# Transposed weights woven into the attention epilogue, and loads split into pieces: a pre-norm layer on eight cores

## What is computed

```python
x = x + attn(layernorm(x))     # x is [4, 4096, 1024] fp32
x = x + ffn(layernorm(x))

def attn(x, w_qkv, w_fc, b_fc, gamma, beta):
    q, k, v = split(x @ w_qkv.T)
    att = softmax(q @ k.T / 32)
    y = einsum('bqk,bvd->bqd', att, v)        # k and v are summed apart
    h = x + y @ w_fc.T + b_fc
    return layernorm(h) * gamma + beta

def ffn(x, w_gate, w_up, w_down):             # inner size 4096
    gate = silu(bitlinear(x, w_gate)); up = bitlinear(x, w_up)
    return bitlinear(gate * up, w_down)
# bitlinear: weights rounded to -1, 0, 1 times mean(|w|); activations to 8-bit integers per row
```

## Time and profile before

| | us |
|---|---|
| median of 2 runs | 4026.79 (4022.05 to 4031.53) |
| the profiled execution | 4026.35 |
| its span, slowest core (core 4) | 4024.8 |
| spans of the eight cores | 4006.8 to 4024.8 |
| VectorE busy | 1588.0 |
| TensorE busy | 856.0 |

### The profile page before, as it was taken

One profiled execution on the slowest core, in us unless ns is written; L12 is line 12 of the kernel. 1 busy time (PEld: TensorE's weight loads), 2 busy tenths in 40 slices (PEclk: granted clock), 3 DMA queues, 4 the chain that ended last, 5 costly groups with the idle time before them and its releaser, 6 DMA issues.

```text
span 4024.8 us, 21432 instructions; the slowest of 8 cores (4006.8 to 4024.8 us)
## 1 busy us (share of the span) xinstructions
PE 856.0 (21%) x3852; PEld 430.0 (11%) x3852; DVE 1588.0 (39%) x3100; ACT 278.4 (7%) x378; POOL 259.1 (6%) x392
## 2 busy tenths in 40 slices
PE   1222200000000300000000047019015900591066
PEld 1222200000000000000000013004002400240022
DVE  5555433333333100024447764713830373037400
ACT  0000000000000000000000023103100310031000
POOL 1111110000000000024430000000000000000000
PEclk9999999999999755555555568559558955895588
DMA  4444443335333475321111142044025402550244
GB/s 129 154 146 136 148 149 108 106 107 136 102 102 97 107 174 149 97 67 42 52 43 46 42 120 84 32 107 123 21 78 158 130 21 68 142 157 21 58 128 128
DMA packets 387523, 404.15 MB, mean 100 GB/s; under 512 B 240961, under 2 KB 306497, under 8 KB 383298
## 3 DMA queue, kind: packets, MB, share of 16 engines
q1 hardware_dynamic: 222210, 163.65, 15.0%
q10 hardware_dynamic: 149760, 176.19, 14.8%
q0 software_dynamic: 15424, 62.93, 4.1%
HBM read 251.67 MB, written 96.47 MB: 86 GB/s over the span
## 4 chain that ended last, share of the span: by engine, by line
DVE 33%; DMA 32%; PE 15%; issue 7%; SPq 6%; ACTq 3%; POOL 2%; DVEq 1%; ACT 1%; POOLq 0%
DVE AR L35 16%; PE pb L35 15%; DVE p0scr L35 7%; SPq L35 5%; DMA wstg<-w_down 5%; DMA wstg<-w_up 5%; DMA AR<-s_wd2t 5%; DMA wstg<-w_gate 4%; DVE svec L35 4%; DMA AR<-s_wd 3%; ACTq L35 2%; POOL AR L35 2%; DMA s_x<-AR 2%; DVE p0f L35 2%; DMA s_wd2t<-AR 2%
## 5 line engine op out<-in xcount | busy, mean ns | idle before, releaser
L35 PE MATMUL pb<-AR 128*128 128x512 bf16 (+1 forms) x3072 | 700.6, 386 | 1898.7 <-DMA AR<-s_wg2t 1222.5
L35 PEld LDWEIGHTS pb<-AR 128*128 128x128 bf16 (+1 forms) x3072 | 303.0, 99 | 2296.7 <-issue 1980.3
L35 DVE TENSOR_TENSOR AR<-AR 128x1024 f16<-128x1024 f16 (+2 forms) x464 | 295.5, 637 | 456.6 <-ACT AR L35 343.9
L35 DVE TENSOR_SCALAR p0scr<-wstg,tcols 128x1024 bf16<-128x1024 f32 x192 | 144.5, 753 | 456.1 <-DMA wstg<-w_down 159.8
L35 DVE SCALAR_TENSOR_TENSOR AR<-pb,a2d,AR 128x512 f32<-128x512 f32 x32 | 24.0, 750 | 496.7 <-PE pb L35 392.1
L35 PE MATMUL pb<-ones_cf,xstage 128*128 128x1 f32 x512 | 113.4, 351 | 362.2 <-DVE xstage L35 362.2
L35 DVE SCALAR_TENSOR_TENSOR p0f<-wstg 128x512 f32<-128x512 f32 x192 | 132.9, 692 | 102.8 <-DMA wstg<-w_down 30.2
L35 DVE SCALAR_TENSOR_TENSOR svec<-svec 128x1 f32<-128x1 f32 x96 | 16.3, 170 | 357.2 <-ACT svec L35 350.3
L35 PEld LDWEIGHTS pb<-ones_cf,xstage 128*128 128x128 f32 x512 | 111.6, 330 | 363.9 <-issue 363.9
L35 DVE TENSOR_SCALAR AR<-AR 128x1024 f16<-128x1024 f16 x320 | 136.6, 427 | 34.6 <-DVE AR L35 0.9
L35 DVE TENSOR_REDUCE svec<-AR 128x1 f32<-128x512 f16 (+1 forms) x160 | 126.8, 792 | 23.8 <-DMA AR<-s_x 7.1
(11 more groups left out here) (107 smaller groups left out, 737.8 us busy)
## 6 DMA issues: line engine op xcount, KB each, us to landing
wstg<-w_gate ACTq DMA_DIRECT2D x64, 512.0 KB, 3.6
wstg<-w_up ACTq DMA_DIRECT2D x64, 512.0 KB, 3.6
wstg<-w_down ACTq DMA_DIRECT2D x64, 512.0 KB, 4.0
AR<-s_wg2t SPq DMA_DIRECT2D x256, 128.0 KB, 2.6
AR<-s_wu2t SPq DMA_DIRECT2D x256, 128.0 KB, 2.9
AR<-s_wd2t SPq DMA_DIRECT2D x128, 256.0 KB, 2.6
AR<-x_full POOLq DMA_DIRECT2D x32, 512.0 KB, 6.2
AR<-s_x SPq DMA_DIRECT2D x32, 512.0 KB, 3.9
```

What stands on the lines that cost most here:

```text
L35: return getattr(E, meth)(*args, **kw)
```

## The change

Three things. First, stage 5 is no longer recorded ahead of the epilogue. A function `rt_emit(n)` records the next n of 64 items on ScalarE's queue, and it is called with 4 at the end of each of the 16 epilogue tiles. An item is half a gate or up block (2 transposes of [1024, 128], one 512 KB store) or one down block. Two slots are used in turn, with semaphores of their own (`qTR0/1` for the transposes, `qTS0/1` for the stores), and an item's first transpose waits for the store of the item two before. The waits on the finished weights become waits on both `qTS` counts. The load of the first activation transposes on SP waits for them too.

Second, each 512 KB load of the FFN weights (stages 1 and 3) and of w_qkv and w_fc (stage 2) becomes four DMAs of 256 columns, 128 KB each, on the same queue and the same semaphore. Third, each 512 KB load of x (stages 1 and 6) and of x1 (stage 7 and the end of each FFN block) becomes two DMAs of 512 columns. Stage 3, stage 2 and the x1 loads are changed as the two shown.

```diff
@@ -230,8 +230,13 @@
             waits = []
             if idx >= 2:
                 waits.append(("vV", p0b_abs[idx - 2]))
-            ld = b.dma("scalar", f"qA{slot}", mk("dma_start", out=stg, in_=w3_tile(m, j)),
-                       waits=waits)
+            src = w3_tile(m, j)
+            ld = None
+            for q4 in range(4):
+                ld = b.dma("scalar", f"qA{slot}",
+                           mk("dma_start", out=stg[:, q4 * 256:(q4 + 1) * 256],
+                              in_=src[:, q4 * 256:(q4 + 1) * 256]),
+                           waits=waits if q4 == 0 else ())
             aw = [(f"qA{slot}", ld)]
             if idx >= 2:
                 aw.append(("gC", 2 * (idx - 2) + 2))
...
@@ -336,8 +347,11 @@
             t_idx = g * 4 + i
             xt = AR4[:, i * 1024:(i + 1) * 1024]
             w = [("vV", e_norm_done[t_idx - 4])] if t_idx >= 4 else []
-            b.dma("gpsimd", "qP1X", mk("dma_start", out=xt,
-                                       in_=x_hbm[t_idx * 128:(t_idx + 1) * 128, :]), waits=w)
+            for q2 in range(2):
+                b.dma("gpsimd", "qP1X",
+                      mk("dma_start", out=xt[:, q2 * 512:(q2 + 1) * 512],
+                         in_=x_hbm[t_idx * 128:(t_idx + 1) * 128, q2 * 512:(q2 + 1) * 512]),
+                      waits=w if q2 == 0 else ())
         grp_total = b.cnt["qP1X"]
         for i in range(4):
             xt = AR4[:, i * 1024:(i + 1) * 1024]
...
@@ -534,36 +552,50 @@
         bank_gate[2 + eh] = ("vV", e_colfc)
     e_p2_tensor = b.cnt["tM"]
 
-    rtA = AR3[:, 5120:9216]
-    rtB = rtA[:, 0:1024].bitcast(F16)
-    e_rt_st = None
-    for mtx, src, dst in ((0, s_w3[0], s_wg2t), (1, s_w3[1], s_wu2t)):
-        for ds in range(8):
+    rt_slots = [AR3[:, 5120:7168], AR3[:, 7168:9216]]
+    rt_items = ([("gu", mtx, ds, half) for mtx in (0, 1) for ds in range(8)
+                 for half in range(2)] +
+                [("wd", ic, 0, 0) for ic in range(32)])
+    rt_state = {"i": 0, "st": {}}
+
+    def rt_emit(n):
+        while rt_state["i"] < len(rt_items) and n > 0:
+            i = rt_state["i"]
+            kind, a1, a2, a3 = rt_items[i]
+            sl = i % 2
+            slot = rt_slots[sl]
             lw = []
-            if mtx == 0 and ds == 0:
+            if i == 0:
                 lw += [("qAS0", e_qas_all[0]), ("qAS1", e_qas_all[1]),
                        ("tM", e_p2_tensor)]
-            if e_rt_st is not None:
-                lw.append(("qTR1", e_rt_st))
-            ldr = None
-            for q in range(4):
-                ldr = b.dma("scalar", "qTR0",
-                            mk("dma_start", out=rtA[:, q * 1024:(q + 1) * 1024],
-                               in_=src[q * 1024:(q + 1) * 1024, ds * 128:(ds + 1) * 128],
-                               transpose=True), waits=lw if q == 0 else ())
-            e_rt_st = b.dma("scalar", "qTR1",
-                            mk("dma_start", out=dst[ds * 128:(ds + 1) * 128, :], in_=rtA),
-                            waits=[("qTR0", ldr)])
-    e_rt_wgwu = e_rt_st
-    for ic in range(32):
-        ldr = b.dma("scalar", "qTR0",
-                    mk("dma_start", out=rtB, in_=s_w3[2][:, ic * 128:(ic + 1) * 128],
-                       transpose=True),
-                    waits=[("qTR1", e_rt_st)])
-        e_rt_st = b.dma("scalar", "qTR1",
-                        mk("dma_start", out=s_wd2t[ic * 128:(ic + 1) * 128, :], in_=rtB),
-                        waits=[("qTR0", ldr)])
-    e_rt_all = e_rt_st
+            if i >= 2:
+                lw.append((f"qTS{sl}", rt_state["st"][i - 2]))
+            if kind == "gu":
+                src = s_w3[a1]
+                dst = s_wg2t if a1 == 0 else s_wu2t
+                ldr = None
+                for q in range(2):
+                    ldr = b.dma("scalar", f"qTR{sl}",
+                                mk("dma_start", out=slot[:, q * 1024:(q + 1) * 1024],
+                                   in_=src[a3 * 2048 + q * 1024:a3 * 2048 + (q + 1) * 1024,
+                                           a2 * 128:(a2 + 1) * 128],
+                                   transpose=True), waits=lw if q == 0 else ())
+                st = b.dma("scalar", f"qTS{sl}",
+                           mk("dma_start",
+                              out=dst[a2 * 128:(a2 + 1) * 128, a3 * 2048:(a3 + 1) * 2048],
+                              in_=slot), waits=[(f"qTR{sl}", ldr)])
+            else:
+                sl16 = slot[:, 0:1024].bitcast(F16)
+                ldr = b.dma("scalar", f"qTR{sl}",
+                            mk("dma_start", out=sl16,
+                               in_=s_w3[2][:, a1 * 128:(a1 + 1) * 128],
+                               transpose=True), waits=lw)
+                st = b.dma("scalar", f"qTS{sl}",
+                           mk("dma_start", out=s_wd2t[a1 * 128:(a1 + 1) * 128, :],
+                              in_=sl16), waits=[(f"qTR{sl}", ldr)])
+            rt_state["st"][i] = st
+            rt_state["i"] += 1
+            n -= 1
 
     gbrow = fcB[0:1, 0:1024]
     e_gamld = b.dma("gpsimd", "qMB", mk("dma_start", out=gbrow, in_=gam_hbm[:, :]),
...
@@ -629,8 +661,12 @@
         xw = [("vV", e_cast_last)]
         if qt >= 2:
             xw.append(("vV", prev_ep[qt - 2]["x_done"]))
-        ld_x = b.dma("sync", f"qXT{qslot}",
-                     mk("dma_start", out=xt, in_=x_hbm[qt * 128:(qt + 1) * 128, :]), waits=xw)
+        ld_x = None
+        for q2 in range(2):
+            ld_x = b.dma("sync", f"qXT{qslot}",
+                         mk("dma_start", out=xt[:, q2 * 512:(q2 + 1) * 512],
+                            in_=x_hbm[qt * 128:(qt + 1) * 128, q2 * 512:(q2 + 1) * 512]),
+                         waits=xw if q2 == 0 else ())
         lw = [(f"qXT{qslot}", ld_x), ("vV", e_fcbc)]
         ev_ln1t = b.op("vector", mk("tensor_scalar", ln1t, xt, mu1[:, qt:qt + 1], r1c[:, qt:qt + 1],
                                     Alu.subtract, Alu.mult), inc="vV", waits=lw)
...
@@ -675,7 +711,11 @@
         b.dma("gpsimd", "qGX1", mk("dma_start", out=s_x1[qt * 128:(qt + 1) * 128, :], in_=hbuf),
               waits=[("vV", ev_x1)])
         prev_ep[qt] = {"x_done": ev_x1}
-
+        rt_emit(4)
+
+    rt_emit(64)
+    e_rt_wgwu = [("qTS0", rt_state["st"][30]), ("qTS1", rt_state["st"][31])]
+    e_rt_all = [("qTS0", rt_state["st"][62]), ("qTS1", rt_state["st"][63])]
     e_p3_tensor = b.cnt["tM"]
     e_p3_v = b.cnt["vV"]
     e_p3_g = b.cnt["gP"]
...
@@ -764,7 +808,7 @@
             ed5 = b.dma("gpsimd", "qMB", mk("dma_start", out=s_dbg[:, 4096:5120], in_=g2b))
             b.wait("vector", "qMB", ed5)
         b.op("vector", mk("scalar_tensor_tensor", g1b, g1b, -1.0, g2b, Alu.add, Alu.add), inc="vV")
-        qw2 = [("qGQ1", 16 * tt)] if tt >= 1 else [("qTR1", e_rt_all)]
+        qw2 = [("qGQ1", 16 * tt)] if tt >= 1 else list(e_rt_all)
         ev_q = b.op("vector", mk("scalar_tensor_tensor", xqo, g1b, 1.0, r0b, Alu.mult, Alu.add),
                     inc="vV", waits=qw2)
         e_q1[tt] = ev_q
...
@@ -801,6 +845,7 @@
             w.append(("tM", e_gu_done[k - 2]))
         if k == 0:
             w.append(("tM", e_p3_tensor))
+            w += e_rt_all
         last = None
         for ds in range(8):
             last = b.dma("sync", f"qQ1T{sl}",
...
@@ -824,7 +869,7 @@
             wsl = dc % 2
             wload_w = []
             if k == 0 and dc <= 1:
-                wload_w.append(("qTR1", e_rt_wgwu))
+                wload_w += e_rt_wgwu
             if k == 0 and dc == 0:
                 wload_w.append(("tM", e_p3_tensor))
             prev_key = (k, dc - 2) if dc >= 2 else ((k - 1, 6 + dc) if k > 0 else None)
...
```

More of the change, by code:

```diff
@@ L29 @@
                              "qWU", "qQ2T", "qWD", "qA", "qAS", "qGLN", "qGQs",
-                             "qGN", "qGO") for i in (0, 1)])
+                             "qGN", "qGO", "qTS") for i in (0, 1)])
 def mk(meth, *args, **kw):
@@ L301, in p0c_tiles @@
                 lw.append(("vV", p0c_state["signB"][idx - 2]))
-            ld = b.dma("scalar", f"qA{slot}", mk("dma_start", out=stg, in_=w3_tile(m, j)), waits=lw)
+            src = w3_tile(m, j)
+            ld = None
+            for q4 in range(4):
+                ld = b.dma("scalar", f"qA{slot}",
+                           mk("dma_start", out=stg[:, q4 * 256:(q4 + 1) * 256],
+                              in_=src[:, q4 * 256:(q4 + 1) * 256]),
+                           waits=lw if q4 == 0 else ())
             wA = [(f"qA{slot}", ld), ("vV", scale_ready[m])]
@@ L415, in build_program @@
             waits.append(("vV", e_cast[idx - 2]))
-        ld = b.dma("sync", f"qWN{slot}", mk("dma_start", out=stg, in_=src[j * 128:(j + 1) * 128, :]),
-                   waits=waits)
+        ld = None
+        for q4 in range(4):
+            ld = b.dma("sync", f"qWN{slot}",
+                       mk("dma_start", out=stg[:, q4 * 256:(q4 + 1) * 256],
```

(20 more changed lines are left out.)

## The result

| | before | after |
|---|---|---|
| median, us | 4030.55 (8 runs) | 3865.03 (9 runs, 3845.72 to 3879.56) |
| ratio to before | | 0.959, 95% interval 0.957 to 0.961 |
| span of the profiled execution | 4024.8 | 3866.1 |
| forecast | | 3737, range 3655 to 3815 |

The change makes the kernel 4.1% faster, where 7% was forecast, and the time lies 50 us above the range. The sign, and the term that was to bring the gain, hold; 128 us of the gain are missing.

A forecast was written before the change was run, and what follows sets the result against it. No single engine bounds it: transposes (364 us) and epilogue (353 us) run one after the other, and load landings are exposed. 4026.35 - 333.87 + 16 + 3 + 14 + 7 + 4 = 3736.5, about 3737 us; range 3655 to 3815.

The forecast's parts named there:

- the wait for the first square root: Before the epilogue: VectorE's 333.87 us wait on ScalarE goes, as the square root precedes the first transpose item.
- first eight epilogue tiles: Epilogue with gate/up items: period 24.0 us, between 22.2 and 25.3, against 22.06 before; 8 x 2.0 = +16 us.
- last eight: Epilogue with w_down items: only the s_x store can be late, +0.4 us x 8 = +3 us.
- quantization in pieces: Weight quantization: four pieces land +0.15 us later per tile than one load, paid 96 times, +14 us.
- first pass in pieces, x in halves: First weight pass: half the piece delay, 48 x 0.15 = +7 us; x halves +0.5 us for 8 groups, +4.
- Rival (e): Epilogue: the square root is still released late because items hold the queue; 4051 us, chance 0.01.
- the line through them gives 2.15: Split loads: lower landing estimate for a 128 KB piece, from 256 KB at 2.6 us and 512 KB at 3.5.
- I take +0.15, near the lower estimate: Split loads: the delay per tile chosen from +0.05 to +0.4 us, with -0.2 allowed as lower bound.
- Rival (a) in its milder form: Split loads: pieces land late, +0.4 us per tile, +58 instead of +21, 3774 us; chance 0.18 including 0.03 for full form.
- The weight 48 for the first pass: First weight pass: with two loads in flight only half the piece delay is paid, 48 x 0.15 = +7 us.
- Rival (c): Epilogue: load and store of items don't overlap, four items take 30.5 us, +68 instead of +16; 3789 us, chance 0.10.
- Both signs that the prediction named for being wrong: Tiles of the first two passes change by over 0.5 us; transposes slow by more than 3.1 us of other traffic per period.

The follow-up runs named there:

- The added load of the experiment: One more 512 KB x load on SP's queue per epilogue tile, added to the kernel with woven transposes and whole loads: 3778.1 us, 0.938 of before.

## Why the prediction was wrong

Against 4026.35 us, each term of the sum, us:

| term | forecast | measured |
|---|---|---|
| the wait for the first square root | -334 | -334: 1411.58 us with whole loads, as its input before |
| first eight epilogue tiles | +16 | 222.6 - 8 x 22.06 = +46 |
| last eight | +3 | 188.0 - 176.5 = +12 |
| quantization in pieces | +14 | +77 (811 against 734); 61 come back with whole loads |
| first pass in pieces, x in halves | +7 and +4 | +38 (626 against 588); on the average of the cores 30 for the pieces, 12 for the halves |

**The stall: right.** The square root was released as read from program order, nothing took the stall's place at one point (the longest wait for a square root is 5.3 us), and the stages behind kept their length. Rival (e) is out.

**The split loads: the term that failed.** Of the 128 us missing, 90 are here and 39 in the epilogue; without the 90 the time would have been inside the range, without the 39 it would not. The step was "the line through them gives 2.15" and "I take +0.15, near the lower estimate, because the four pieces arrive on otherwise idle engines". A landing was priced by a line through two sizes of different tensors (w_down's transposed rows on SP at 256 KB, w_gate at 512 KB), and the piece was put where the line had it. Measured on the slowest core, a 128 KB piece of these tiles takes 2.7 to 3.0 us although the DMA engines are only 36% busy in the quantization, and even the upper end, 2.5, taken from another tensor and queue, was too low; w_gate's pieces had it on six of the eight cores, those of all three weights only on cores 4 and 5 (2.5, 2.5 and 2.6 us). With the stagger of 1.37 us VectorE waits longer for a tile by 0.7 us (w_gate), 0.9 (w_up) and 0.8 (w_down), beyond the +0.4 that the range allowed. Rival (a) in its milder form was the right one, at twice its price; its sentence "a landing is mostly fixed" held.

The Trainium skill's rule ("DMA: Bandwidth & Descriptors", section "Anatomy of one DMA — SWDGE (gpsimd) path"), a fixed 2.0 us per DMA plus the bytes, gave an estimate of +0.5 per tile: nearer than the line, still below the 0.7 to 0.9 of the runs. That section states its fit for DMAs that GpSimd issues, and these loads go out on ScalarE's queue, so the prediction borrowed it.

The weight 48 for the first pass was about right: on the average of the cores the weight pieces cost 30 us there and 52 in the quantization, 0.32 and 0.55 us per tile, so with two loads in flight a little over half of the delay is paid. The x halves cost 12 us where 4 were forecast, inside their range. The 7.2 us that the prediction gives for a quantization tile is that of w_gate; the average was 7.6 (734/96), which changes nothing in the sum.

**The epilogue: mechanism right, size too small.** I took 24.0 us per period between 22.2 and 25.3; it was 27.8. Of the 5.6 us over 22.2, about 2 are what other traffic does to the third item (8.5 us on average against 6.6 for the second). The rest was left out of the sum: with the neighbouring item's store beside it an item takes 6.0 to 6.6 us instead of 5.4, four times per period, and the s_x store, delayed by transposes, makes VectorE wait longer. Even with the queue relieved the period stays at 26.1. The added load of the experiment cost 1.6 us per period, about the whole of its own engine time. That agrees with the Trainium skill ("DMA: Bandwidth & Descriptors", section "Issuing engines are not separate DMA queues"): DMAs issued by different engines run on the same 16 DMA engines and interleave.

The sentence "no row of before shows a transpose beside another queue's transfer" was wrong for the trace. Transposes of the same shape, [1024, 128], stand on SP's queue beside the quantization's loads:

```profile
AR<-s_wqkv SPq DMA_TRANSPOSE x8, 4.6
```

They land after 4.6 us, against 3.2 for a w_down transpose with nothing beside it (each has a second one issued 1.5 us behind it, so not all of the difference need be the other queue's).

I had counted the engines' work as 20.1 of 22 us and not drawn the consequence that with engines 91% booked the landings would not keep the values they had one at a time. Rival (c), no overlap at all (30.5 us), is refuted: the items before and behind the third follow each other in 6.0 to 6.6 us on average, not 7.6.

Both signs that the prediction named for being wrong came true: a quantization tile changed by 0.8 us, over the 0.5, and the period grew by 5.6 us, more than the 3.1 of other traffic.

**The sentence that missed the larger thing.** I read correctly that each load stands behind the previous tile's store, "its landing wholly exposed, 96 times", and priced only what the change would add to it. The order of these two records was worth 325 us.

## What to carry to other kernels

A DMA cut into pieces on one queue ends at about (pieces - 1) issues plus the landing of one piece, and the landing of a quarter was here three quarters of the whole (2.7 against 3.6 us); cut only where something consumes the pieces one by one or the landing is covered. Where a queue's instructions wait, look at what is recorded behind them: two stalls here went by a new order, one of 334 us together with smaller items and a second slot, one of 325 us by reordering alone. When two stages are overlapped, add up their DMA time per period; where it comes near the whole period, as here (20.1 of 22 us), the waits can move to whichever transfer is on the critical loop, as they did to the s_x store. Look at all cores: a transfer whose landing varies costs what it costs on the slowest.

## What the runs showed of the hardware

- For [128 x 1024] fp32 tiles loaded on ScalarE's queue, the median landing (w_gate, slowest core) was 3.6 us for 512 KB, 3.1 for 256 KB and 2.7 for 128 KB, with four issues 0.46 us apart. Pieces with runs of 4 KB and of 1 KB in DRAM landed alike (2.9 and 2.7 us).
- The landing of whole tiles in the quantization was the same on all cores within 0.1 us (w_gate, w_up) or 0.3 us (w_down). That of 128 KB pieces differed between pairs of neighbouring cores, 2.5 to 3.1 us for w_up, and was alike within a pair; cores 2 and 3 were the slowest pair in one kernel and the fastest in another.
- DMA transposes and another queue's transfers slow each other: an s_x store of 512 KB landed after 4.9 us without transposes and 6.9 beside them (at worst, with four slots and mixed items, VectorE waited 12.1 us for it), and two transposes with their store went from 5.4 us to 8.5 on average, 9.2 at most, beside an x load and that store.
- 512 KB loads two deep with 256 KB stores ran at 194 GB/s on the slowest core with all eight at it, the DMA engines 71% busy, and landed in about 4.5 us (w_up, w_down) instead of 3.6 to 4.1.
